# Macaron block: another table of jobs per slot, and another order in the prologue

## The reference

```
x = x + 0.5 * ffn(layernorm(x))     # ffn: FFT along channels, complex matrix, real part of inverse FFT, + bias
x = x + attention(layernorm(x))     # on the left 128 channels, 16 heads of 8, scale 1/4, softmax over keys, out @ Wo.T + bo
x = x + 0.5 * ffn(layernorm(x))
```

## Time and profile before

| | us |
|---|---|
| runs of the kernel before | 317.94, 313.4, 312.87 (median 313.4) |
| the profiled execution | 312.38 |
| its span, first to last instruction | 310.5 |
| granted TensorE clock in it | 1.0 in all 40 slices |

### The profile page before, as it was taken

How to read it: one execution, slowest core, us unless ns; L and a number is a source line. 1 busy time by engine, 2 the same in 40 slices (tenths; PEclk the granted TensorE clock), 3 DMA queues, 4 the chain that set the end, 5 groups by cost and what they waited for, 6 DMA issues and landing times.

```text
span 310.5 us, 8810 instructions
## 1 busy us (share of the span) xinstructions
PE 294.8 (95%) x3440; PEld 112.5 (36%) x3443; DVE 190.5 (61%) x552; ACT 257.6 (83%) x285; POOL 98.3 (32%) x113
## 2 busy tenths in 40 slices
PE   8887999899998999999999999999999999998996
PEld 5633333233332333333333333334333333322333
DVE  1688546747775678657776678567755643370255
ACT  2117998898997889998998989998999999999921
POOL 6562531223604053223604251313600340034005
PEclk9999999999999999999999999999999999999999
DMA  7935615573462762665453663554372464112102
GB/s 192 337 137 192 218 65 153 195 270 133 139 217 83 245 208 103 208 204 217 155 192 129 231 205 112 198 172 143 131 238 104 138 205 170 38 68 70 37 34 70
DMA packets 25891, 49.33 MB, mean 159 GB/s; under 512 B 2032, under 2 KB 14192, under 8 KB 24048
## 3 DMA queue, kind: packets, MB, share of 16 engines
q1 hardware_dynamic: 25152, 48.26, 46.0%
q10 hardware_dynamic: 688, 0.40, 0.8%
HBM read 31.08 MB, written 17.56 MB: 157 GB/s over the span
## 4 chain that ended last, share of the span: by engine, by line
PE 75%; DMA 9%; DVE 5%; ACT 5%; issue 3%; POOL 3%; SPq 0%; ACTq 0%; POOLq 0%
PE ot L828 28%; PE misc L719 26%; PE scores L799 15%; ACT probs L669 5%; DMA leftT<-left_scr 4%; DMA q_scr<-qp 2%; PE scores L719 2%; DMA QS<-q_scr 2%; DMA left_scr<-left_blocks 1%; POOL x L553 1%; PE scores L686 1%; PE scores L693 1%; DVE left_blocks L966 1%; DVE lh L957 1%; POOL rstd L550 1%
## 5 line engine op out<-in xcount | busy, mean ns | idle before, releaser
L669 ACT ACTIVATE probs<-scores 128x1024 f32<-128x1024 f32 x256 | 243.8, 1028 | 20.6 <-PE scores L799 20.3
L828 PE MATMUL ot<-probs,VS 128*32 128x512 f32 x1024 | 133.9, 594 | 2.9 <-ACT probs L669 2.3
L799 PE MATMUL scores<-QS,KS 32*128 32x512 f32 x512 | 64.7, 495 | 3.0 <-DMA QS<-q_scr 1.3
L799 PEld LDWEIGHTS scores<-QS,KS 32*128 32x128 f32 x512 | 24.5, 181 | 109.8 <-ACT probs L669 101.0
L828 PEld LDWEIGHTS ot<-probs,VS 128*32 128x32 f32 x1024 | 30.6, 109 | 25.8 <-ACT probs L669 5.0
L563 POOL TENSOR_TENSOR x_out<-x,half_bias 128x512 f32<-128x512 f32 x7 | 9.0, 1292 | 88.8 <-DVE x L1012 88.8
L548 POOL TENSOR_SCALAR veps<-mv 128x4 f32<-128x4 f32 (+1 forms) x25 | 6.1, 242 | 95.9 <-DVE mv L946 95.9
L1017 DVE SCALAR_TENSOR_TENSOR x_out<-misc,rstd,x_out 128x256 f32<-128x256 f32 x28 | 13.5, 484 | 33.7 <-PE misc L719 30.2
L719 PE MATMUL misc<-half_ffn,xT 128*32 128x256 f32 x448 | 32.1, 386 | 0.0
L719 PE MATMUL misc<-half_ffn,xT_in 128*32 128x256 f32 x400 | 27.1, 385 | 1.4 <-DVE half_ffn L1193 1.3
L550 POOL TENSOR_TENSOR rstd<-veps,power 128x4 f32<-128x4 f32 (+1 forms) x25 | 25.3, 1013 | 2.1
(11 more groups left out here) (125 smaller groups left out, 260.0 us busy)
## 6 DMA issues: line engine op xcount, KB each, us to landing
KS<-k_scr SPq DMA_DIRECT2D x14, 512.0 KB, 4.9
QS<-q_scr SPq DMA_DIRECT2D x14, 512.0 KB, 4.6
x_in<-x SPq DMA_DIRECT2D x8, 512.0 KB, 5.1
xT_in<-x_t SPq DMA_DIRECT2D x8, 512.0 KB, 6.4
k_scr<-kp SPq DMA_DIRECT2D x8, 512.0 KB, 3.0
q_scr<-qp SPq DMA_DIRECT2D x8, 512.0 KB, 4.4
x_scr<-x_blocks SPq DMA_DIRECT2D x7, 512.0 KB, 2.9
xT<-x_scr SPq DMA_DIRECT2D x7, 512.0 KB, 4.7
```

The lines of the kernel that those rows point to most:

```text
L669: nc.scalar.activation(probs[u % PRING][:, :, :], scores[u % SRING][:, :, :], ACT.Exp, scale=SCORE_SCALE).then_inc(exp_done, 1)
L799: last = mm(scores[(u + j // 2) % SRING][:, j % 2, :], KS[b % 2][rows, slot, kt * P:(kt + 1) * P].bitcast(F32R), QS[b % 2][rows, slot, :]. ...
L828: last = mm(ot[COL * j:COL * (j + 1), :], VS[b % 2][:, kt, h, :], probs[(u + j // 2) % PRING][:, j % 2, :], start=s % 8 == 0, stop=s % 8 == 7)
```

## The change

The tables are written anew: k of the next batch is computed in slots 4 and 6 of the batch before (STEADY), and no more two batches ahead in slots 14 and 15; values stand in 5 and 7, q in 8 and 9 instead of 7 and 8, N in 11 instead of 10, F1 ends in slot 10 instead of 6, and F2_3 begins in slot 15. For batches 1 and 2 k is still computed in batch 0 (for 2 now in its slots 14 and 15), so FIRST has no k, and LATE has k for batch 7. left_half, turn_left and the guard move back accordingly, the first statistics of a later batch forward. SyncE's order becomes x2, k_out, k_in, q_out, q_in, then left_through. In the prologue half_bias, two bias rows, and half of batch 1's statistics come earlier; the second norm of batch 0 is done in two halves; and the last F1 of batch 1 is evacuated after KT and QT. Four semaphores are added for it.

```
@@ -66,28 +66,31 @@
-STEADY = {0: [("F2_3a", -2, LEFT), ("F2_3", -2, LEFT)], 1: [("F1_0a", 2, LEFT), ("F1_0", 2, LEFT)],
+STEADY = {0: [("F2_3", -2, LEFT), ("F1_0a", 2, RIGHT)], 1: [("F1_0", 2, RIGHT)],
           2: [("WO_0", -1, LEFT), ("WO_1", -1, RIGHT)], 3: [("WO_2", -1, LEFT), ("WO_3", -1, RIGHT)],
-          4: [("F1_1a", 2, LEFT), ("F1_1", 2, LEFT)], 5: [("F1_2a", 2, LEFT), ("F1_2", 2, LEFT)],
-          6: [("F1_3a", 2, LEFT), ("F1_3", 2, LEFT)], 7: [("QT_0", 1, LEFT)], 8: [("QT_1", 1, LEFT)],
-          9: [("V_0", 1, RIGHT), ("V_1", 1, LEFT)], 10: [("N", 1, RIGHT), ("F2_0a", -1, LEFT)], 11: [("F2_0", -1, LEFT)],
-          12: [("F2_1a", -1, LEFT), ("F2_1", -1, LEFT)], 13: [("F2_2a", -1, LEFT), ("F2_2", -1, LEFT)],
-          14: [("KT_0", 2, RIGHT)], 15: [("KT_1", 2, RIGHT)]}
-
-FIRST = {**STEADY, 0: [("F1_0a", 2, LEFT), ("F1_0", 2, LEFT)], 1: []}
+          4: [("KT_0", 1, RIGHT), ("F1_1a", 2, LEFT)], 5: [("F1_1", 2, LEFT), ("V_0", 1, RIGHT)],
+          6: [("KT_1", 1, RIGHT), ("F1_2a", 2, LEFT)], 7: [("F1_2", 2, LEFT), ("V_1", 1, RIGHT)], 8: [("QT_0", 1, RIGHT)],
+          9: [("QT_1", 1, RIGHT), ("F1_3a", 2, LEFT)], 10: [("F1_3", 2, LEFT)],
+          11: [("N", 1, RIGHT), ("F2_0a", -1, LEFT)], 12: [("F2_0", -1, LEFT), ("F2_1a", -1, RIGHT)], 13: [("F2_1", -1, RIGHT)],
+          14: [("F2_2a", -1, LEFT), ("F2_2", -1, LEFT)], 15: [("F2_3a", -1, LEFT)]}
+
+FIRST = {**STEADY, 0: [("F1_0a", 2, LEFT), ("F1_0", 2, LEFT)], 1: [("F1_1a", 2, LEFT), ("F1_1", 2, LEFT)],
+         4: [("F1_2a", 2, LEFT)], 5: [("F1_2", 2, LEFT), ("V_0", 1, RIGHT)], 6: [("QT_0", 1, RIGHT)], 7: [("QT_1", 1, RIGHT)],
+         8: [("F1_3a", 2, LEFT)], 9: [("F1_3", 2, LEFT)], 10: [("V_1", 1, RIGHT)]}
 BEGIN = {3: [("LT", 1, LEFT)], 4: [("KT_0", 1, RIGHT), ("F1_0a", 2, LEFT)], 5: [("F1_0", 2, LEFT), ("QT_0", 1, RIGHT)],
          6: [("KT_1", 1, RIGHT), ("F1_1a", 2, LEFT)], 7: [("F1_1", 2, LEFT), ("QT_1", 1, RIGHT)],
-         8: [("F1_2a", 2, LEFT), ("F1_2", 2, LEFT)], 9: [("F1_3a", 2, LEFT), ("F1_3", 2, LEFT)],
-         10: [("V_0", 1, RIGHT), ("V_1", 1, LEFT)], 11: [("N", 1, RIGHT)], 12: [("LT", 2, LEFT)],
-         13: [("KT_0", 2, RIGHT)], 14: [("KT_1", 2, LEFT)]}
-
-LATE = {0: [("F2_3a", -2, LEFT), ("F2_3", -2, LEFT)],
+         8: [("F1_2a", 2, LEFT), ("F1_2", 2, LEFT)], 9: [("V_0", 1, RIGHT), ("F1_3a", 2, LEFT)],
+         10: [("F1_3", 2, LEFT), ("N", 1, RIGHT)], 11: [("V_1", 1, RIGHT)],
+         13: [("LT", 2, LEFT)], 14: [("KT_0", 2, RIGHT)], 15: [("KT_1", 2, RIGHT)]}
+
+LATE = {0: [("F2_3", -2, LEFT)],
         2: [("WO_0", -1, LEFT), ("WO_1", -1, RIGHT)], 3: [("WO_2", -1, LEFT), ("WO_3", -1, RIGHT)],
-        5: [("QT_0", 1, LEFT)], 6: [("QT_1", 1, LEFT)], 7: [("V_0", 1, RIGHT)], 8: [("V_1", 1, LEFT)],
-        9: [("F2_0a", -1, LEFT)], 10: [("F2_0", -1, LEFT), ("N", 1, RIGHT)], 11: [("F2_1a", -1, LEFT)], 12: [("F2_1", -1, LEFT)],
-        13: [("F2_2a", -1, LEFT)], 14: [("F2_2", -1, LEFT)]}
-END = {0: [("F2_3a", -2, LEFT), ("F2_3", -2, LEFT)],
+        4: [("KT_0", 1, RIGHT)], 5: [("KT_1", 1, RIGHT)], 6: [("QT_0", 1, RIGHT)], 7: [("QT_1", 1, RIGHT)],
+        8: [("V_0", 1, RIGHT)], 9: [("V_1", 1, RIGHT), ("F2_0a", -1, LEFT)], 10: [("F2_0", -1, LEFT), ("N", 1, RIGHT)],
+        11: [("F2_1a", -1, LEFT)], 12: [("F2_1", -1, LEFT)],
+        13: [("F2_2a", -1, LEFT)], 14: [("F2_2", -1, LEFT)], 15: [("F2_3a", -1, LEFT)]}
+END = {0: [("F2_3", -2, LEFT)],
        2: [("WO_0", -1, LEFT), ("WO_1", -1, RIGHT)], 3: [("WO_2", -1, LEFT), ("WO_3", -1, RIGHT)],
        9: [("F2_0a", -1, LEFT)], 10: [("F2_0", -1, LEFT)], 11: [("F2_1a", -1, LEFT)], 12: [("F2_1", -1, LEFT)],
        13: [("F2_2a", -1, LEFT)], 14: [("F2_2", -1, LEFT)], 15: [("F2_3a", -1, LEFT), ("F2_3", -1, LEFT)]}
@@ -103,7 +106,7 @@
         ahead = [(f"F1_{t}", 2) for t in range(T)]
-        jobs = [(f"F1_{t}", 1) for t in range(T)] + [("LT", 1)] + ahead + [("KT", 1), ("QT", 1), ("N", 1)]
+        jobs = [(f"F1_{t}", 1) for t in range(T)] + [("LT", 1)] + ahead[:-1] + [("KT", 1), ("QT", 1), ahead[-1], ("N", 1)]
@@ -126,7 +129,7 @@
 def guard_slot(it):
-    return 12 if it else 13
+    return 13 if 0 < it < B - 2 else 12
@@ -500,31 +507,26 @@
             k_out(1)
+            q_out(1)
             k_in(1)
-            q_out(1)
...
             for it in range(1, B):
-                if it + 1 < B:
-                    k_out(it + 1)
...
                     load_x(it + 3)
-                if it + 1 < B:
-                    k_in(it + 1, slice(0, 1))
                 x2_through(it - 1)
-                if it + 1 < B:
-                    k_in(it + 1, slice(1, None))
...
                 if it + 1 < B:
+                    k_out(it + 1)
+                    k_in(it + 1)
                     q_out(it + 1)
+                    q_in(it + 1)
...
                     left_through(it + 2)
-                if it + 1 < B:
-                    q_in(it + 1)
+                store_out(it - 1, 0)
...
                     leftT_in(it + 2)
-                store_out(it - 1, 0)
@@ -581,15 +583,19 @@
                 add_rows(x_in[b % 2], x_in[b % 2], half_bias, xb_done)
-            rstd_of(0, 1)
...
             add_row(x1[0], x_in[0], half_bias, early_biased, slice(1, 2))
+            rstd_of(0, 1)
...
             add_rows(x1[1], x_in[1], half_bias, xb_done)
-            rstd_of(1, 1)
+            pool.wait_ge(first_mv, 1)
+            nc.gpsimd.tensor_scalar(veps[1][:, 0:2], mv[1][:, 0:2, 1], EPS, None, ALU.add).then_inc(first_veps, 1)
+            pool.wait_ge(first_veps, 1)
+            nc.gpsimd.tensor_tensor(rstd[1][0][:, 0:2], veps[1][:, 0:2], power[:, 0:2], ALU.pow).then_inc(first_rstd, 1)
+            rstd_of(1, 1, slice(2, T))
@@ -629,12 +635,12 @@
                 nc.scalar.copy(copy[:, :, :], half_bank(bank)).then_inc(ffn_copied, 1)
+            act.wait_ge(bias_loaded, 16)
+            nc.scalar.mul(half_bias[:, :], bias_raw[:, :], 0.5).then_inc(bias_set, 1)
...
                 nc.scalar.mul(copy[:, :, :], half_bank(bank), 0.5 / E).then_inc(ffn_copied, 1)
-            act.wait_ge(bias_loaded, 16)
-            nc.scalar.mul(half_bias[:, :], bias_raw[:, :], 0.5).then_inc(bias_set, 1)
@@ -660,9 +666,9 @@
                 if it + 1 < B:
-                    if s == (2 * 4 if it else 2 * 8):
+                    if s == (2 * 7 if it == B - 2 else 2 * 8):
                         square(kp, sq_k, kp_step, it + 1)
-                    if s == (2 * (8 if it == B - 2 else 10) if it else 2 * 9):
+                    if s == (2 * 11 if 1 < it < B - 2 else 2 * 9):
@@ -952,7 +958,8 @@
             def left_half(b, tiles=range(T)):
-                dve.wait_ge(rstd_done[1], b + 1)
+                if b or tiles[-1] == T - 1:
+                    dve.wait_ge(rstd_done[1], b + 1)
@@ -1202,20 +1209,41 @@
             fold(half_ffn, even[2], odd[:, :, :], ALU.subtract, ALU.add, 6, 4)
-            for s in range(T):
-                run_jobs(PROLOGUE, s)
-            norm0_stats(1)
-            left_half(0)
+            dve.wait_ge(mv_done[0], 1)
+            norm0_stats(1, range(0, 2))
+            def first_x1(t):
+                dve.wait_ge(evacuated, evac_count(f"F1_{t}", 0))
+                return nc.vector.bn_stats(stats[1][:, t, :], x1[0][:, t, :])
+            evacuate("F1_0", 0)
+            evacuate("F1_1", 0)
+            first_x1(0)
+            evacuate("F1_2", 0)
+            first_x1(1).then_inc(first_stats, 1)
+            dve.wait_ge(first_stats, 1)
+            for t in range(2):
+                last = nc.vector.bn_aggr(mv[1][:, t, :], stats[1][:, t, :])
+            last.then_inc(first_mv, 1)
+            evacuate("F1_3", 0)
+            first_x1(2)
+            first_x1(3).then_inc(stats_done[1], 1)
+            norm_moments(1, 1, range(2, T))
+            dve.wait_ge(first_rstd, 1)
+            left_half(0, range(0, 2))
+            norm0_stats(1, range(2, T))
+            left_half(0, range(2, T))
             norm_moments(0, 2)
-            run_jobs(PROLOGUE, T)
-            for t in range(T):
+            evacuate("LT", 0)
+            for t in range(T - 1):
                 evacuate(f"F1_{t}", 1)
-            run_jobs(PROLOGUE, 2 * T + 1)
-            run_jobs(PROLOGUE, 2 * T + 2)
+            evacuate("KT", 0)
+            evacuate("QT", 0)
+            evacuate(f"F1_{T - 1}", 1)
...
             nc.vector.tensor_copy(KS[0][:, 0, :].bitcast(F32R), row_banks[0]).then_inc(first_k_set, 1)
-            run_jobs(PROLOGUE, 2 * T + 3)
+            evacuate("N", 0)
@@ -1248,16 +1276,16 @@
                     if it + 2 < B:
-                        if s == (8 if it else 10):
+                        if s == 12:
                             left_half(it + 2, range(0, 2))
-                        if s == (9 if it else 10):
+                        if s == (13 if it else 12):
...
                     if it + 3 < B:
-                        if s == 11:
+                        if s == 6:
                             norm0_stats(it + 3, range(0, 2))
```

(6 more changed lines are left out.)

## The result

The changed kernel takes 317.11 us (median of six runs, 315.98 to 318.89), the kernel before beside it 312.56 (six runs, 310.87 to 317.94). The ratio is 1.0147, with an interval of 1.0095 to 1.0199: some 4.6 us slower. The forecast was 311.5, and its range ended at 315.5. The profiled execution of after is the slowest of its six, 318.89 with a span of 317.0; the spans of the others lie between 314.1 and 315.7.

The account below looks back on a forecast made before the run. TensorE, busy 95% of the span, sets the pace in batches 2 to 5, ScalarE in 6 and 7. Prologue -0.75, batch 0 -0.45, batch 1 -1.4, batches 2 to 5 +0.7: -1.9, median 311.5; own range 310.7 to 312.4, over all cases 309.0 to 315.5.

Parts of the forecast that it names:

- VectorE, GpSimd, the guard: VectorE's work, at most 2.3 us per slot in slots of 2.29, and the guard's move were costed at nothing.
- rival D: VectorE falls behind in slots 4 to 9, delaying k, q and TensorE by 0.5 per batch: 313.5; chance 0.08.
- without that cover 0.1 to 0.3 per batch: Cost if k's evacuation in slot 6 does not end some 0.25 before slot 7's jobs; costed at nothing.
- Batches 6 and 7 and the tail nothing: No change there, ScalarE being the limit; half a us either side for q and squares in LATE's slots.
- rival A: q's rows come 0.85 us or more late in each of batches 2 to 5; at 1.5, 316.1; chance 0.2.
- Batches 2 to 5, +0.7: Waits for q's rows 4 x 0.35 = 1.4, small waits -0.3, half a job out of batch 5 -0.43.
- The prologue: Earlier half_bias and bias rows and the halved second norm bring the first value quad forward: -0.75 us.
- a mark for being wrong: The prologue step counts as wrong if GpSimd's first half rstd ends after 18.0.
- Batch 0: Slots from quad 10 on -1.35, against a new 0.9 wait for lh before batch 2's LT: -0.45 us.
- Batch 1: Wait for leftT gone -1.48, one half job fewer -0.43, squares in slots 6 to 10 +0.5: -1.4 us.

Follow-up runs that it names:

- a2: The changed kernel with q stored ahead of k_in in iteration 6 alone: 314.53 us, ratio 1.0078.
- a3: The changed kernel with the edits of a1 and a2 together: 312.34 us, ratio 1.0018.
- a1: The changed kernel with GpSimd waiting for left_half before next_x's bias additions for batches 4 to 7: 317.17 us, ratio 1.0143.
- b2: The kernel before with two extra, unused GpSimd additions where left_half runs, in iterations 1 to 5: 317.99 us, ratio 1.0181.
- d1: c1 with GpSimd's wait for left_half before next_x's additions holding for batch 3 too: 310.79 us, ratio 0.9935.
- b1: a3 with q stored ahead of k_in in iteration 1 as well as 6: 311.63 us, ratio 0.9961.
- c1: b1 with VectorE doing F1_3's statistics and moments between N's first reduction and its judging operations, in batch 0 alone: 311.73 us, ratio 0.999.
- b4: b1 with the prologue of the kernel before: 312.52 us, ratio 1.0013.
- c3: b1 unchanged, run again beside c1 and c2: 311.09 us, ratio 0.9976.
- a4: The kernel before with the changed kernel's prologue alone: 312.99 us, ratio 1.0024.
- c2: The kernel before, its tables untouched, with the new prologue and q_out(1) ahead of k_in(1) in batch 0's queue: 311.03 us, ratio 0.9961.

## Why the prediction was wrong

The forecast was -1.9 and after came out at +4.6. What failed are two steps that were priced at nothing. The other terms held in size once these were mended, one of them because two errors cancelled.

**"VectorE, GpSimd, the guard", failed.** I counted VectorE's instructions by their durations in the trace of before, and there left_half never ran beside an addition of GpSimd's. The change moved left_half to slots 12 and 13, where next_x adds its rows. I named the two engines in one heading and laid their timelines side by side nowhere. The price is 0.8 in each of batches 2 to 4 of the trace (35.3 to 35.4, where the repaired kernels take 34.5 without a wait for QS), and some 2.2 in the medians (a2 against a3). The sign of this step was rival D's, VectorE late, but D had put it in slots 4 to 9, for lack of room, at 0.5. a1, b2 and d1 show the cause; the Trainium skill's rule on the shared ports ("SBUF — State Buffer", "Who interferes with whom") spoke against the change and was not weighed. The same step failed a second time, and here by D's own mechanism: "without that cover 0.1 to 0.3 per batch" stood in the forecast, the cover wasn't there, and slot 8 costs 0.3 in each of batches 2 to 5. No run repairs it.

**"Batches 6 and 7 and the tail nothing", failed.** I had rival A's mechanism, q late behind k, and worked it out for batches 2 to 5, whose slots 4 to 9 keep k and q apart. LATE has k in slots 4 and 5 and q in 6 and 7. There q is ready 2.3 us before k_in's wait ends and 3.5 before its own store goes out, since the queue holds it. Iteration 1 has the same fault: k_out stands behind x2's way, so it leaves at 76.69. The price is 4.8 in the trace of after: 3.0 for the wait, 1.0 for the quad behind it at the lower clock, and 0.6 that a2 keeps without any wait (31.78 against 31.16). The 0.6 lie where two more half jobs (18 and not 16; the forecast gave back one) and the squares stand, which I had put behind ScalarE; no run takes them apart. In the medians the order of the queue is worth 2.6 (a2). The store's time was wrong too: the forecast took 3 to 4 us for k's. In iterations 1 and 6, where it follows xT's transfer within 0.7 us, it took 5.7 and 5.6. The Trainium skill, "DMA: Bandwidth & Descriptors", section "Anatomy of one DMA", has a fit of 2.0 us plus bytes over 436 GB/s, made on transfers that GpSimd issues. An estimate from it is 3.2 for 512 KB. For SyncE's stores it doesn't hold here: they took 2.8 to 7.1.

**Batches 2 to 5, +0.7: right by luck.** QS was to be late by 0.35 in each. After has none of it. With GpSimd's additions out of the way it is 0.18 in one batch of a3, 0.38 and 0.43 in b1, 0.24 and 1.93 in c1, 1.01 in d1, and under 0.2 or none in a1, b4 and c3. Over these seven executions that is 0.15 per batch, less than half of the forecast, and it is a spread from one execution to the next and no constant. Against that stands slot 8, 0.3 per batch, which the sum had at nothing. So the four batches together come out 0.9 above before in the mean of the seven traces, and 0.2 in c3, which has no wait for QS, where the forecast without these waits said -0.7.

**The prologue, right in the traces but for one.** Forecast -0.75, measured -1.0 to -1.1 from the first F1 product to the first value quad in nine of the ten traces with the new prologue. The tenth, a3, has +0.4, and the forecast had no term for that: a wait for the bias row in front of the copies, and the lower clock behind it. In the runs the prologue isn't settled: b1 and b4 differ by 0.9 as forecast, a4 shows no gain over before. I had set a mark for being wrong, the first half rstd ending after 18.0. It ended at 18.23, and the step was right all the same, since in this execution the first F1 product started 0.83 later. A mark has to be counted from an event of the same chain.

**Batch 0, right.** Forecast -0.45, measured -0.43, with 0.93 for the new wait where 0.9 was written. Half of the reason stood: N's chain ahead of the statistics delays lh. c1 shows that this alone isn't it, d1 that without the chain and without GpSimd's additions 0.36 is left.

**Batch 1, right in size once both faults are gone.** Forecast -1.4, after -0.83, b1 -1.42, d1 -1.43. The rest in after is norm_max at 2.27, with 0.53 of TensorE's time behind it. In a1, a2 and a3, with the queue of after, it also waited for QS by 2.72, 0.75 and 0.94.

**The total.** With both faults repaired the new kernel takes 311.6, 311.1 and, with d1's two edits, 310.8, where 311.5 was forecast. That looks better than it is, for the forecast started from 313.4, the median of three runs. Against before as it ran beside them b1 and c3 gain 1.2 and 0.8 by their ratios, where 1.9 was forecast; d1 gains 2.0. The intervals reach from 0.2 to 2.2 for b1 and up to 1.7 for c3, so that the runs don't show whether the rest of the sum was worth its 1.9 or half of it. c2 shows, too, that as much is to be had without the new tables. What d1 gains over c2 is not beyond the intervals.

Left open: why a1's median shows nothing of a gain that its trace has. Four runs with 4 us between them don't decide it. That the freed time went into waits for QS, as in the profiled one, is likely and not shown for the others. What speaks for it is the mean granted clock: in a1's profiled execution it is 0.989, and 0.994 to 0.995 in the other three, and the two traces of after and a1 show each long wait for QS followed by a lower clock. Three of after's six runs and all of a2's have 0.999 or 1.0.

## What to carry to other kernels

When a stage of one engine is moved, lay the other engines' timelines beside its new place before pricing it, GpSimd's beside VectorE's above all: durations read from the old place don't move with it. In a queue with waits, ask for each iteration and each special table whether something ready stands behind a wait for something else; the regular batches say nothing of the first and the last. When a wait for a transfer is moved ahead of work that everything hangs on, price the execution in which it lands late. And where a round trip through memory has a margin smaller than the spread of its landing times, count a part of that spread as cost.
